# The second attention's front for two batches, moved into the first routed experts' last blocks

## What is computed

```
x = layernorm(x + L0_attn(x))     # 16 heads of 64, half-causal mask, projections Wq Wk Wv Wo
x = layernorm(x + L0_ffn(x))      # 8 experts, the 2 best of each token, silu(x gate) * (x up), then down
x = layernorm(x + L1_attn(x))     # 16 heads of 8: c_k = x w_dk, c_v = x w_dv, k = c_k w_uk, v = c_v w_uv,
                                  # q = x; rotary position on q and k; softmax; w_o
x = layernorm(x + L1_ffn(x))      # 8 routed experts (2 best) and 2 shared ones, gelu
```

## Time and profile before

| | |
|---|---|
| median of 3 runs | 1343.99 us |
| profiled execution | 1343.33 us |
| its span, first to last instruction | 1341.5 us |
| granted TensorE clock, mean | 0.978 |
| TensorE matmul, weight load busy | 1252.5 us (93%), 1070.9 us (80%) |
| VectorE, ScalarE, GpSimd busy | 976.9 us (73%), 921.5 us (69%), 618.2 us (46%) |
| first attention | 0 to about 560 us |
| first routed experts | about 560 to 747 us |
| second attention | from 749.9 us |

### The profile page before, as it was taken

One profiled execution on the slowest core, in us unless ns is written; L12 is line 12 of the kernel. 1 busy time (PEld: TensorE's weight loads), 2 busy tenths in 40 slices (PEclk: granted clock), 3 DMA queues, 4 the chain that ended last, 5 costly groups with the idle time before them and its releaser, 6 DMA issues. The chain is left out here.

```text
span 1341.5 us, 34497 instructions
## 1 busy us (share of the span) xinstructions
PE 1252.5 (93%) x10783; PEld 1070.9 (80%) x10784; DVE 976.9 (73%) x2973; ACT 921.5 (69%) x2434; POOL 618.2 (46%) x967
## 2 busy tenths in 40 slices
PE   6999999999999999999999489999999998869996
PEld 5888888888888887899999367777777776658985
DVE  6777788788878888766666488898989887363443
ACT  4777777777777776656665367878778786758863
POOL 3244444444444443453343524556556552336773
PEclk9999999999999999999999679999999999999998
DMA  8012212121202021021111522022115101113326
GB/s 267 21 53 69 67 52 75 45 85 35 91 28 92 28 88 58 15 71 57 56 54 38 190 92 77 22 89 86 43 65 174 49 17 45 60 33 106 110 73 198
DMA packets 56445, 99.82 MB, mean 74 GB/s; under 512 B 11184, under 2 KB 46384, under 8 KB 53744
## 3 DMA queue, kind: packets, MB, share of 16 engines
q1 hardware_dynamic: 45840, 78.58, 18.5%
q0 software_dynamic: 9088, 18.89, 4.2%
q10 hardware_dynamic: 1440, 1.39, 0.3%
HBM read 77.85 MB, written 62.06 MB: 104 GB/s over the span
## 5 line engine op out<-in xcount | busy, mean ns | idle before, releaser
L326 ACT ACTIVATE a_prob<-psum,a_nmx 128x128 f32<-128x128 f32 (+1 forms) x512 | 208.3, 425 | 82.4 <-DVE a_nmx L631 82.4
L530 POOL TENSOR_TENSOR a_prob<-a_prob,a_rl 128x128 f32<-128x128 f32 (+1 forms) x256 | 124.3, 508 | 244.1 <-DVE a_rl L635 243.5
L2373 DVE TENSOR_REDUCE a_nmx<-psum 128x2 f32<-128x512 f32 x256 | 170.1, 685 | 22.0 <-PE psum L1658 19.2
L333 ACT ACTIVATE a_probt<-psum 128x768 f32<-128x768 f32 x128 | 105.1, 821 | 70.8 <-PE psum L961 70.8
L2030 ACT ACTIVATE a_prob<-psum 128x1024 f32<-128x1024 f32 x128 | 127.3, 1024 | 7.5 <-PE psum L1688 7.3
L1658 PE MATMUL psum<-k_stk,a_q_stk 96*128 96x256 f32 x512 | 116.1, 320 | 12.8 <-DVE a_nmx L2373 8.6
L577 POOL DMA_INDIRECT yt<-a_yrow,a_dest x78 | 75.2, 964 | 101.3 <-ACT a_yrow L373 87.1
L1658 PEld LDWEIGHTS psum<-k_stk,a_q_stk 96*128 96x128 f32 x512 | 78.3, 194 | 43.3 <-issue 18.3
L326 ACT ACTIVATION_READ_ACCUMULATOR a_prob<-psum,a_nmx 128x1 f32 x512 | 107.8, 211 | 0.0
L961 PE MATMUL psum<-ident,a_prob 128*128 128x128 f32 x768 | 106.1, 274 | 1.4 <-DVE a_prob L641 1.0
L620 DVE TENSOR_TENSOR a_qkt<-psum,a_bqk 128x512 f32<-128x512 f32 x128 | 88.2, 689 | 21.7 <-PE psum L103 21.3
(11 more groups left out here) (385 smaller groups left out, 3859.6 us busy)
## 6 DMA issues: line engine op xcount, KB each, us to landing
xs<-in_fill SPq DMA_DIRECT2D x144, 264.0 KB, 4.3
a_xrow<-xs SPq DMA_DIRECT2D x39, 132.0 KB, 2.1
m_xrow<-xs SPq DMA_DIRECT2D x39, 132.0 KB, 2.2
w<-in_w SPq DMA_DIRECT2D x16, 256.0 KB, 3.5
a_yin<-yt SPq DMA_DIRECT2D x16, 256.0 KB, 2.6
f_yin<-yt SPq DMA_DIRECT2D x7, 512.0 KB, 8.2
w<-in_wr SPq DMA_DIRECT2D x2, 1284.0 KB, 7.7
xs<-in_fill_idle SPq DMA_DIRECT2D x2, 1056.0 KB, 6.6
```

The costliest lines, as they stand in the source:

```text
L326: last = nc.scalar.activation(prob[:, hp % 4, h, at], S[:, 2 * (hp % 2) + h, at], ACT.Exp, bias=nmx[:, hp % 4, q, h:h + 1], accum_out=lsum ...
L333: nc.scalar.activation(probt[:, hp % 2], PT[:, :, 0:SW], ACT.Copy).then_inc(pt_done, 1)
L530: last = nc.gpsimd.tensor_tensor(prob[:, hp % 4, 0, at], prob[:, hp % 4, 0, at], rl[:, hp % 4, 0, q:q + 1].to_broadcast(prob[:, hp % 4, 0, ...
L2373: nc.vector.reduce_max(nmx[:, :, h:h + 1], bank.rearrange("p (q k) -> p q k", q=QB), AX.X, negate=True).then_inc(mx_done, 1)
```

## The change

1. The front of batches 0 and 1 (up to the keys' sine product of batch 1) is taken out of the second attention and put into `attention0_routed0`. Each engine gets a function `front_step(j)` behind `block_step(j, ...)` for j from 24 on. The front's tiles and semaphores live in both stages (`front_buffers`), the helpers are shared (`front_tensor`, `front_scalar`, `front_gpsimd`, `front_vector`). Blocks 8 to 23 are looped, 24 to 38 written out. The constants and the selector are loaded by SyncE behind the row load of block 23, the expert rows of batches 0 and 1 behind the row load of block 31, and the fill of the second `xs` region goes behind the last row load.
2. The transposed columns of the blocks from 8 on go to bank 6, the front works in bank 7.
3. The late part of the block table is made over 16 parts instead of 8 experts: at first up to two blocks (NEXT_BLOCKS) of each expert, then the rest, so that the first 24 blocks hold the rows of the first batches.
4. The router's logits go to `TC` in the score banks for all batches but the last. TensorE then waits for the current pair's exponentials ahead of the router, and for the logits' read one period later.
5. In the second attention ScalarE's markers for batch 0 come behind its stacks, and the markers for batch 1 behind the first two stacks of batch 1.

The core of the diff; what is left out are the moved helpers, whose bodies are the same as before, and declarations:

```diff
+    FRONT_BLOCKS = SLOTS * 3
+    LOOPED_BLOCKS = range(SLOTS, FRONT_BLOCKS)
...
-        bank = 2 + j if isinstance(j, int) and j in (0, 1) else 7
+        bank = 6 if not isinstance(j, int) or j >= SLOTS else 7 if j > 1 else 2 + j
...
+            for dst, src in ((f.small32[:], d["small"]), (f.bias[:], d["a1_bias"]), (f.in_head[:], d["in_head"]),
+                             (f.wu[:, 0, :], d["w_uk"]), (f.wu[:, 1, :], d["w_uv"]), (f.wu[:, 2, :], d["w_o"]),
+                             (f.cos[:], d["cos"]), (f.sin[:], d["sin"])):
+                sp.dma_start(dst, src).then_inc(f.loaded, 16)
+            sp.dma_start(sel32[:], d["sel"]).then_inc(f.sel_in, 16)
+            for j in range(LOOPED_BLOCKS.stop, NB):
                 sp.wait_ge(y_out[j % SLOTS], j // SLOTS * 32)
                 block_rows(j, j % SLOTS)
+                if j == FRONT_BLOCKS + SLOTS - 1:
+                    for m in range(2):
+                        sp.dma_start(f.yin[:, m], g.yt[m * 2 * T:(m + 1) * 2 * T].rearrange("(q p k) f -> p q k f", p=P, k=2)
+                                     ).then_inc(f.y_in[m], 16)
+            sp.dma_start(g.next_xs[IDLE:XROWS].rearrange("(p r) f -> p (r f)", p=P), d["fill_idle"]).then_inc(f.filled, 16)
+            for e in range(E1):
+                sp.dma_start(g.next_xs[e * STRIDE:e * STRIDE + GT].rearrange("(p r) f -> p (r f)", p=P), d["fill"][e]).then_inc(f.filled, 16)
...
+            def front_step(j):
+                if j == 24:
+                    nc.scalar.activation(f.th[:], g.gap[:], ACT.Tanh, scale=0.5).then_inc(f.th_done, 1)
+                if j == 30:
+                    incoming1(columns_of(0), 1)
+                if j == 31:
+                    act.wait_ge(f.loaded, f.LOADS * 16)
+                    latents1(0, 1)
+                if j == 32:
+                    keys1(1)
+                if j == 34:
+                    incoming1(columns_of(1), 2)
+                if j == 35:
+                    latents1(1, 2)
+                if j == 36:
+                    keys1(2)
...
+            def front_step(j):
+                if j == 24:
+                    nc.gpsimd.memset(f.halfs[:], -0.5).then_inc(f.set, 1)
+                    pool.wait_ge(f.set, 1)
+                if j == 25:
+                    pool.wait_ge(f.pr_done, 1)
+                    weigh_rows1(0, 0, 16)
+                if j == 27:
+                    incoming_power1(1)
+                if j == 28:
+                    weigh_rows1(1, 1, 16)
+                if j == 30:
+                    pool.wait_ge(f.loaded, f.LOADS * 16)
+                    pool.wait_ge(f.rx_done, 1)
+                    rotate_x1(columns_of(0), 1, 1)
+                    incoming_power1(2)
+                if j == 31:
+                    rotate_k1(1)
+                if j == 34:
+                    pool.wait_ge(f.rx_done, 2)
+                    rotate_x1(columns_of(1), 2, 2)
+                if j == 35:
+                    rotate_k1(2)
...
+                chain.done(nc.vector.tensor_scalar(t.parts[:, 0:E0], t.blocks[:], float(NEXT_BLOCKS), None, ALU.min))
+                chain.done(nc.vector.tensor_tensor(t.parts[:, E0:], t.blocks[:], t.parts[:, 0:E0], ALU.subtract))
...
+            def late_before():
+                n = 2 * E0
+                chain.done(nc.vector.tensor_tensor(t.below2[:], t.parts[:].unsqueeze(1).to_broadcast([P, n, n]),
+                                                   rc2[:, n:].rearrange("p (a b) -> p a b", a=n), ALU.mult))
+                chain.done(nc.vector.reduce_sum(t.upto2[:], t.below2[:], AX.X))
+                chain.done(nc.vector.tensor_tensor(t.skip2[:], t.parts[:], t.upto2[:], ALU.subtract))
+                chain.done(nc.vector.scalar_tensor_tensor(t.start2[:], t.skip2[:], float(BR), t.first2[:], ALU.mult, ALU.add))
...
+                chain.done(nc.vector.tensor_tensor(t.done2[:], wide2(t.upto2[:]), entries2(rc("jj")[:, 0:n]), ALU.is_le))
+                chain.done(nc.vector.reduce_sum(t.part[:], t.done2[:], AX.X))
+                nc.vector.tensor_tensor(t.done2[:], wide2(rc2[:, 0:2 * E0]), entries2(t.part[:]), ALU.is_equal)
+                chain.done(nc.vector.tensor_scalar(t.fold[:], t.part[:], float(E0) - 0.5, -float(E0), ALU.is_gt, ALU.mult))
+                chain.done(nc.vector.tensor_tensor(expert[:, late], t.part[:], t.fold[:], ALU.add))
...
+            def front_step(j):
+                if j == 25:
+                    dve.wait_ge(f.th_done, 1)
+                    chain.done(nc.vector.memset(f.pr[:], 0.0))
+                    nc.vector.tensor_scalar(f.pr[:, 0:NTL, 0], f.th[:], 0.5, 0.5, ALU.mult, ALU.add)
+                    nc.vector.tensor_scalar(f.pr[:, 0:NTL, 1], f.th[:], -0.5, 0.5, ALU.mult, ALU.add).then_inc(f.pr_done, 1)
+                if j == 26:
+                    dve.wait_ge(f.loaded, f.LOADS * 16)
+                    chain.done(nc.vector.tensor_copy(f.wd_h[:], f.small32[:, 0:2, :]))
+                    nc.vector.tensor_tensor(f.wd_l[:], f.small32[:, 0:2, :], f.wd_h[:].bitcast(F32), ALU.subtract)
+                    nc.vector.tensor_copy(f.rot[:], f.small32[:, 2, :]).then_inc(f.consts, 1)
+                if j == 27:
+                    dve.wait_ge(f.sel_in, 16)
+                    nc.vector.tensor_copy(f.sel[:].rearrange("p a k n -> p (a k n)"), sel32[:]).then_inc(f.sel_done, 1)
+                if j == 28:
+                    incoming_variances1(1)
+                if j == 29:
+                    incoming_rows1(1)
+                if j == 30:
+                    incoming_low1(columns_of(0), 1)
+                if j == 31:
+                    incoming_variances1(2)
+                if j == 32:
+                    rotate_q_first1(1)
+                    incoming_rows1(2)
+                if j == 33:
+                    rotate_k_first1(1)
+                    rotate_q_rest1(1, True)
+                if j == 34:
+                    incoming_low1(columns_of(1), 2)
+                    rotate_k1(1, True)
+                if j == 36:
+                    rotate_q_first1(2)
+                if j == 37:
+                    rotate_k_first1(2)
...
+            def front_step(j):
+                if j == 30:
+                    incoming1(1)
+                if j == 31:
+                    pe.wait_ge(f.loaded, f.LOADS * 16)
+                    pe.wait_ge(f.consts, 1)
+                    pe.wait_ge(f.rx_done, 1)
+                    latents1(columns_of(0), 1)
+                if j == 32:
+                    keys1(columns_of(0), 1)
+                if j == 33:
+                    pe.wait_ge(f.k_done, 1)
+                    pe.wait_ge(f.xsin_done, 1)
+                    turn1()
+                if j == 34:
+                    pe.wait_ge(f.ksin_done, 1)
+                    incoming1(2)
+                if j == 35:
+                    pe.wait_ge(f.rx_done, 2)
+                    latents1(columns_of(1), 2)
+                if j == 36:
+                    keys1(columns_of(1), 2)
+                if j == 37:
+                    pe.wait_ge(f.k_done, 2)
+                    pe.wait_ge(f.xsin_done, 2)
+                    turn1()
...
+                if u == 0 and batch > 1:
+                    pe.wait_ge(lg_done, i - 1)
...
                     pe.wait_ge(rk_done, i - 1)
                 if u == 3 and batch > 0:
-                    if more:
-                        pe.wait_ge(qk_done, s + 3)
+                    pe.wait_ge(exp_done, s * 2 + 2)
                     router(i)
-                    turn(s - 1, before_hp + 1)
-                    pe.wait_ge(lg_done, i)
...
-            pe.wait_ge(init, 1)
-            incoming(1)
-            pe.wait_ge(loaded, LOADS * 16)
-            pe.wait_ge(consts, 1)
-            pe.wait_ge(rx_done, 1)
-            latents(columns_of(0), 1)
-            pe.wait_ge(consts, 2)
-            keys(columns_of(0), 1)
-            incoming(2, PV)
-            pe.wait_ge(k_done, 1)
-            pe.wait_ge(xsin_done, 1)
-            turn()
-            pe.wait_ge(rx_done, 2)
-            latents(columns_of(1), 2, PV)
-            pe.wait_ge(ksin_done, 1)
-            values(0)
-            pe.wait_ge(sel_done, 1)
+            pe.wait_ge(f.sel_done, 1)
             pe.wait_ge(q_split, 1)
             pe.wait_ge(k_split, 1)
             stack(0, R0)
             stack(1, R1)
-            keys(columns_of(1), 2, PV)
+            pe.wait_ge(ksin_done, 2)
+            values(0)
             pe.wait_ge(stack_act, 1)
             stack(2, R0)
             pe.wait_ge(stack_dve, 1)
             stack(3, R1)
-            pe.wait_ge(k_done, 2)
-            pe.wait_ge(xsin_done, 2)
-            turn(PV)
             pe.wait_ge(stack_act, 3)
...
             nc.scalar.activation(warm[:], g.ident[:, 0:HG], ACT.Exp)
+            stacks(0, 0, R0, 1)
+            stacks(2, 0, R0, 1)
+            stacks(3, 0, R1, 1)
             act.wait_ge(pick_done, 1)
             markers(0)
-            act.wait_ge(init, 1)
-            incoming(columns_of(0), 1)
```

(17 more changed lines are left out.)

491 lines of the change are left out of this document (250 added, 241 removed).

## The result

The changed kernel took 1331.26 us (median of 4 runs, 1329.18 to 1334.02), the kernel before 1345.07 us beside it: a ratio of 0.9908, 95% interval 0.9895 to 0.9921. The forecast was 1331.5. The ratio makes 12.4 us of saving (10.6 to 14.1), where 11.8 was forecast. Measured again on another chip it took 1332.02 us, ratio 0.9900 (0.9883 to 0.9916). The first profiled execution took 1334.02 us (span 1332.1), the slowest of its four; the second one, which I use for the account by stage, had a span of 1330.4.

A forecast was written before the change was run, and what follows sets the result against it. TensorE, busy 93% of the span, bounds the kernel, so a handover can win the middle hole. Terms -15.1 + 4.6 + 2.6 - 3.9 = -11.8 us from 1343.3 gave 1331.5 us; own range 1328.5 to 1334.5, chance 0.60.

The forecast's parts named there:

- Handover: From first routed experts to second attention: first row maximum 10.4 us after stage start instead of 27.6; net 15.1 us saved.
- marker fill: ScalarE's fill for batch 1, now ahead of batch 2's column copy, delays TensorE's latents: 2.1 us of the handover's gain returned.
- two terms ahead of ScalarE's copies: At the new stage's start: 1.5 us for table load and warm activation, about 1.1 us waiting for a low-clock stack.
- Front in the blocks: Front moved into expert blocks: TensorE's moved work 4.1 us for two batches plus 0.5 us of stalls, +4.6 us.
- the stalls: In the front's expert blocks, the weights' split late beyond its 0.96 us of slack: 0.5 us in all, bounds 0 and 4.
- the exclusion: VectorE operations with two SBUF inputs locked out by GpSimd's SBUF reads: 0.74 us excess each, at most one GpSimd operation.
- rival C: Front doesn't fit: VectorE or GpSimd steps delay splits in 13 blocks, 20.8 us instead of 0.5; 1352 us, chance 0.06.
- Block table: Expert blocks 3 to 5, where VectorE is the bound: added table operations are paid, +2.6 us (bounds 1 and 3.5).
- Logits: First attention's loop: 14 weight-load waits for the logits' read go, -3.9 us (bounds 0 and -5).
- B: Everything hides: 19 us from the handover, no block stalls, 1 us for the table; 1325.5 us, chance 0.12.
- A: Handover slower: 11 us saved instead of 15.1, and 1.5 us more of block stalls; 1337 us, chance 0.18.
- D: Front's latency only moves across the barrier, TensorE's steps waiting; logits and table alone remain; 1342 us, chance 0.04.

The follow-up runs named there:

- the run apart: All-early version of the changed kernel, with the split of the front's constants and GpSimd's weighing of batch 1 each one block later: 1323.94 us, ratio 0.9853.
- the one with bank 7: Changed kernel with the transposed columns of blocks 8 to 25 in bank 7, as before the change, instead of bank 6: 1331.39 us.

## Why the prediction was right

The account by stage, kernel before against the second trace of the changed kernel (us): start -0.5; first to fourteenth logits' read -2.9; to block 3's split -0.1; block 3's to block 8's +4.0; to block 27's -0.8; to block 38's +4.9; to the stage's start +0.4; to the first maximum -17.9; to the last maximum +1.6; to the end +0.2. Sum -11.1, the difference of the spans (1330.4 - 1341.5).

- **Handover, -15.1 forecast, -16.3 measured.** The first maximum came 0.8 us sooner than forecast, since the constants had landed earlier and VectorE was never held by them. What was paid back is the marker fill, 2.2 us to the copy's reader against 2.1, and the run without it in the way confirms it. The forecast's two terms ahead of ScalarE's copies came out in size, 1.40 us against 1.5 and 1.10 against 1.1. The cause of the first was wrong: with the table load gone ScalarE still began after 1.37 us, because it waits for TensorE's first stack, beside which the load lay.
- **Front in the blocks, +4.6 forecast, +5.3 measured.** It is +4.9 to block 38's split and +0.4 behind it, where the last turn runs (742.93 in the first trace). The kernel with the same placement and no front is the better measure: against it the front costs 5.4 us to block 38's split and 5.8 in all. In the run apart, without the stalls, it costs 4.1, which is TensorE's own work just as forecast. So the stalls cost 1.7 us where 0.5 was put; 1.11 + 0.25 of it are named waits. The mis-sized term is the exclusion: 0.74 us was taken for one, and 1.47 and 1.53 were measured, more than any of GpSimd's row operations beside them took (0.7 to 1.1 us). That was rival C's mechanism, in two blocks and not in thirteen.
- **Block table, +2.6 forecast.** +2.4 to +2.5 in the three runs where the clock held, +4.0 in both profiles of the changed kernel and in the one with bank 7, where TensorE fell to the lower level behind its 3.07 us. The prediction had no term for the clock.
- **Logits, -3.9 forecast, -2.9 measured.** The named wait disappeared, as forecast; that nothing takes its place was wrong, since 2.1 us of other waits came with it.
- **Start, 0 forecast.** -0.5 in this pair of traces, +2.1 in the first pair: it varies from one execution to the next by more than any price of the edit.
- **Not foreseen: the placement of the buffers,** -0.8 us to block 27 and -1.4 to the stage's start, as the kernel with the same placement and no front shows. It is no part of what the edit does.

So the mechanisms of the four terms were right, but that the number was hit within 0.3 us is luck, by sizes that compensate: the handover 1.2, the placement 1.4 and the start 0.5 better, against the logits 1.0, the stalls 1.2 and the table with the low clock 1.4 worse. The kernel before took 1345.07 beside it and not the 1343.99 that the forecast started from. Of the rivals, B (all hides) failed on the fill, the table and the stalls; A on the handover; D on TensorE's first stack at 0.2 us.

From the port rule of the Trainium skill ("SBUF — State Buffer", the reading of its diagram) the prediction had concluded that a split can be late by one GpSimd operation at most. These traces agree on the exclusion but not on that bound: the subtraction was held 1.47 us beside single row operations of 0.74 to 1.05 us. Whether it was held by one after the other, no run here separates.

## What to carry to other kernels

Read what a moved step will lie beside, not only whether its engine has time: two VectorE steps beside GpSimd's row operations cost 1.7 us, where TensorE's own added work cost 4.1, and one block of distance took it away. When a wait is removed, ask which matmul in the queue is next to wait, and take less than the whole: here 2.9 of 3.9 us. Before crediting an edit that allocates or frees buffers, run the old kernel with a few bytes of padding: part of a gain can be an offset.

## What the runs showed of the hardware

- **The SBUF offset of the experts' buffers changes the rate of matmuls.** With x_h and x_l at offsets of 184,384, 188,032 and 113,056 bytes a partition (the offset is that of x_h) a block lasted 4.87 us; at 113,120 and 184,416 it lasted 4.82 to 4.83 on average. Two of the three groups of matmuls that read them had a mean of 282 and 283 ns against 279, the third (high part of both) 302 in either. The two fast offsets leave 96 in a division by 128, the slow ones 64, 0 and 32. hid moved by the same bytes in each, but its matmuls took 275 ns in either, so it is x_h or x_l; which of them and why is open, and five offsets are no rule.
- **The clock after a stall can differ from one execution to the next.** Behind the same 3.05 to 3.08 us without a matmul, TensorE ran at 1.00 in three executions and fell to the 1.2 GHz level for about 3 us in three others, which cost 1.4 to 1.6 us. In the eight executions whose longest wait there was 1.63 us or less it stayed at 1.00.
- **Landing of scatters at a stage's end.** GpSimd's first instruction of the next stage came 2.80 us after its last scatter instruction where it waited for the landing, 0.95 us where it did not.
